# Two interleaved attentions: router units moved by one step, and within a step, in hand-written unit schedules

## The chip, the cores and the metric

The kernel runs on one core of one Trainium2 chip. The time is the device time of one execution, in microseconds (us). The engines are TensorE (PE in the profile; PEld is its weight load), VectorE (DVE), ScalarE (ACT), GpSimd (POOL) and the DMA-issuing SyncE (SP). Each works through its own instruction list; they meet only in semaphores.

## The reference

Sixteen sequences of 100 tokens with 256 features, and a context of 361 tokens for each, go through four residual blocks:

```python
x = x + tanh(g_xattn[0]) * L0_xattn(layernorm(x), ctx, ctx, mask)     # 16 heads of 16, softmax over 361 keys
x = x + tanh(g_ffn[0])   * L0_ffn(layernorm(x))      # 8 experts, top 2, capacity 1.25: logits, top_k, ranks, gather
x = x + tanh(g_xattn[1]) * L1_xattn(layernorm(x), ctx, ctx, mask2)    # 16 heads of 64, then a layer norm of its own
x = x + tanh(g_ffn[1])   * L1_ffn(layernorm(x))      # 8 experts, top 2 by gates
```

What matters here is that each attention is followed by a routing: normalised rows times router weights give eight logits a token, the two best experts are chosen, and the rank of each token within its expert (a running count over all tokens before it) says in which row of DRAM its features are stored for the expert stage.

## The kernel before

The program is a row of stages: norms, `attention_first` (some 45 to 427 us in the profile), `experts_first`, `attention_second` (some 725 to 1440 us), `experts_second`. Each attention treats eight pairs of batches. A pair is eight **steps** (plus some more in the last pair, where the pipeline runs out). The first pair and the last are written out, pairs 1 to 6 are a hardware loop.

In a step TensorE does the scores of four heads, **turns** (transposes) the four probability tiles of the step before, multiplies those of two steps before with the values (**value**), and, in between, **units**. A unit is one small product into a bank of its own, which another engine then takes away. The order of units is written by hand in `first_schedule` and `second_schedule`: a list of lists `at`, one for each step, with entries (kind, batch 0 or 1 of the pair, tile, part). Part -1 means: for the pair before this one. Kinds: Q, K, V projections; R spreads the softmax inverses, W is the output projection; N, G and C are the three routing units: N transposes the normalised rows (`Router.turn`, L225), G makes the router logits (`Router.score`, L237), C makes the ranks (`Router.rank_rows`, L277 and L278). "none" is an empty unit that makes the number of units a multiple of the banks (two in the first attention, three in the second).

All engines walk the same list. In a step of the first attention (`steps` of each engine) TensorE does: score, turns 0 and 1, value, unit 0, turn 2, unit 1, turn 3, all other units. In the second: score, turn 0, unit 0, turn 1, unit 1, turn 2, unit 2, value, turn 3, all other units. VectorE does four `find_max` (the row minima of the negated scores), then the routing's `moments` where they are due, then copies of finished values and takes the units in their order. Taking G includes `choose`: the maxima, their indices and the one-hot rows (L249 to L261), which C reads. ScalarE makes the exponentials and copies the turned tiles, takes the upper half of Q and K (a rounded copy; `lower` makes the rest), and calls `make_rows` (L215) at the end of the step that the routing is due in: the normalised rows that N transposes. GpSimd's part in the first attention, L1191 to L1211, is for each step: mask conversion, `lower` for each Q and K of the step, `router.scales` (inverse deviation and shift, L206 to L167) if routing is due, then for C `router.route` (15 small operations) and four scatters.

`ROUTE_AT` is the step of the first attention in which moments, scales and rows of the pair before are made (`routed_pair`, L1109). N follows one step later, G two. In the second attention the corresponding constant is `Z_AT`.

Every engine is in order, so a wait in it also holds whatever it has behind the waiting instruction. A score of the first attention also waits until VectorE has copied the value result of the step before (L1578), since both share a bank. A unit waits until the unit that used its bank before is taken.

Of the kernel before, what the change touches and what calls it, by code (L numbers as in the profile page):

```python
# [366 lines left out]
Z_AT = 3  # L367


def second_schedule(last):  # L370

    layer = Layer(1, 64, 1.0 / 16)
    at = [[] for _ in range(STEPS + LAG_VALUE + 5)]
    half = STEPS // 2
    for p in range(half):
        at[p] += [("K", 1, 2 * p, 0), ("K", 1, 2 * p + 1, 0)]
    parts = [(t, p) for t in range(KT_N) for p in range(2)]
    for m, (t, p) in enumerate(parts):  # L380
        at[(1, 1, 3, 3, 4, 4)[m]].append(("V", 1, t, p))
    at[LAG_VALUE].append(("W", 1, 0, -1))
    if not last:
        for p in range(half):
            at[half + p] += [("K", 0, 2 * p, 0), ("Q", 0, 2 * p, 0), ("K", 0, 2 * p + 1, 0), ("Q", 0, 2 * p + 1, 0)]
        for m, (t, p) in enumerate(parts):
            at[half + (1, 1, 2, 3, 3, 3)[m]].append(("V", 0, t, p))
    at[half + LAG_VALUE].append(("W", 0, 0, 0))
    for k, kind in enumerate("NGC"):
        at[Z_AT + 2 + k].insert(0 if kind == "C" else len(at[Z_AT + 2 + k]), (kind, 0, 0, -1))  # L390
    if last:
        at[STEPS + LAG_VALUE].append(("W", 1, 0, 0))
        for k, kind in enumerate("NGC"):
            at[STEPS + LAG_VALUE + 2 + k].append((kind, 0, 0, 0))
        return Units(layer, [u for slot in at for u in slot], at)
    at = at[:STEPS]
    for k in range(-sum(len(slot) for slot in at) % BANKS):
        at[k].append(("none", 0, k, 0))
    return Units(layer, [u for slot in at for u in slot], at)


def attention_second(nc, T, D_):
# [36 lines left out]
    ps_p = [ps(f"ps_p{k}") for k in range(BANKS)]  # L439

    full, final = second_schedule(False), second_schedule(True)
    half = STEPS // 2
    pre = Units(layer, [("Q", 0, t, 0) for t in range(H // 2)] + [("K", 0, t, 0) for t in range(H // 2)]
# [537 lines left out]
QUAD_TURN, QUAD_VALUE = 1, 2  # L981
QUAD_PB, QUAD_PT = 8, 8
FIRST_BANKS = 2
FIRST = 4
ROUTE_AT = 4


def first_schedule(last):

    layer = Layer(0, 16, 0.25)
    at = [[] for _ in range(QUADS + QUAD_VALUE + 5)]
    half = QUADS // 2
    at[0].append(("W", 0, 0, -1))
    at[1] += [("K", 1, 0, 0), ("V", 1, 0, 0)]
    at[2] += [("R", 1, 0, -1), ("V", 1, 1, 0)]
    at[3] += [("K", 1, 1, 0), ("V", 1, 2, 0), ("W", 1, 0, -1)]  # L1000
    at[ROUTE_AT + 1].append(("N", 0, 0, -1))
    at[half + QUAD_VALUE].append(("R", 0, 0, 0))
    at[ROUTE_AT + 2].append(("G", 0, 0, -1))
    if last:
        at[half + QUAD_VALUE + 1] += [("C", 0, 0, -1), ("W", 0, 0, 0)]
        at[QUADS + QUAD_VALUE].append(("R", 1, 0, 0))
        at[QUADS + QUAD_VALUE + 1].append(("W", 1, 0, 0))
        for k, kind in enumerate("NGC"):
            at[QUADS + QUAD_VALUE + 2 + k].append((kind, 0, 0, 0))
        return Units(layer, [u for slot in at for u in slot], at)  # L1010
    at[5] += [("K", 0, 0, 0), ("Q", 0, 0, 0)]
    at[6] += [("V", 0, 0, 0), ("V", 0, 1, 0)]
    at[7] += [("C", 0, 0, -1), ("K", 0, 1, 0), ("Q", 0, 1, 0), ("V", 0, 2, 0)]
    at = at[:QUADS]
    for k in range(-sum(len(slot) for slot in at) % FIRST_BANKS):
        at[ROUTE_AT].append(("none", 0, k, 0))
    return Units(layer, [u for slot in at for u in slot], at)


def attention_first(nc, T, D_):  # L1020
# [32 lines left out]
    ps_p = [ps(f"ps_p{k}") for k in range(FIRST_BANKS)]  # L1053

    full, final = first_schedule(False), first_schedule(True)
    half = QUADS // 2
    pre = Units(layer, [("Q", 0, 0, 0), ("K", 0, 0, 0), ("Q", 0, 1, 0), ("K", 0, 1, 0)]
# [51 lines left out]
    def routed_pair(i, p):  # L1109

        if p == ROUTE_AT:
            return None if isinstance(i, int) and i == 0 else i - 1
# [1481 lines left out]
```

How the kernel before makes its waits and increments, by code:

```python
def wait(eng, counted, i, k):  # L53
    value = counted.at(i, k)
    if not isinstance(value, int) or value > counted.per:
        eng.wait_ge(counted.sem, value)
# [13 lines left out]
    def link(self, eng, ins):  # L71
        eng.wait_ge(self.sem, self.mark(ins))
# [16 lines left out]
    def link(self, eng, ins):  # L89
        eng.wait_ge(self.sem, self.mark(ins))
# [78 lines left out]
    def z_scales(self, pool, j):  # L169
        g, r = self.nc.gpsimd, slice(0, S)
        pool.wait_ge(self.z_averaged.sem, self.z_averaged.at(j, 1))
        self.pool_own.link(pool, g.tensor_scalar(self.dev[r, :], self.mv[r, :, 1], 1e-30, None, ALU.max))
        self.pool_own.link(pool, self.power(self.dev, 0.5))
        self.pool_own.link(pool, g.tensor_scalar(self.rs[r, :], self.dev[r, :], (D / (D - 1.0)) ** 0.5, Z_EPS, ALU.mult, ALU.add))
        self.pool_own.link(pool, self.power(self.rs, -1.0))
        self.make_shift(pool, self.z_scaled)
# [1 line left out]
    def z_rows(self, act, j):  # L179
        act.wait_ge(self.z_scaled.sem, self.z_scaled.at(j, 1))
        self.apart(act)
        for s in range(2):
            z = self.T["xn"][0:S, bass.ds((2 * j + s) * D, D)]
            ins = self.nc.scalar.activation(z, z, ACT.Identity, scale=self.rs[0:S, s:s + 1], bias=self.shift[0:S, s:s + 1])
        ins.then_inc(self.z_done.sem, 1)
# [13 lines left out]
    def scales(self, pool, j):  # L200
# [1 line left out]
        g, r = self.nc.gpsimd, slice(0, S)  # L202
        if j:
            pool.wait_ge(self.dispatched, 64 * j)
        pool.wait_ge(self.averaged.sem, self.averaged.at(j, 1))
```

## Time and profile before

| | |
|---|---|
| median of 3 runs | 1630.07 us (1629.55 to 1630.86) |
| profiled execution, whole | 1641.7 us |
| its span, first to last instruction | 1639.9 us |
| TensorE matmul busy | 1338.0 us (82%) |
| VectorE / ScalarE / GpSimd busy | 876.4 / 802.0 / 409.4 us |
| mean granted TensorE clock | 0.908 of full speed |

Rows of a timeline give start, duration, engine, source line, operation, what is written and read, and how many instructions of the kind are merged; the bracket is the idle time of the engine before it and what ended it. The granted clock is 1.0 at 2.4 GHz; 0.5 is the level of 1.2 GHz.

### The profile page before, as it was taken

How to read it: one execution, taken by the hardware profiler on the slowest of the kernel's cores; microseconds unless marked ns; L12 is line 12 of the kernel's file. 1: busy time of each engine (PE TensorE's matmuls, PEld its weight loads, DVE VectorE, ACT ScalarE, POOL GpSimd, SP SyncE). 2: the span in 40 equal slices, each digit the busy share in tenths (PEclk: the TensorE clock that was granted, in tenths of full speed). 3: DMA queues.
4: the chain of work that ended last, by engine and by line, in shares of the span. 5: the costliest groups of instructions: out<-in, count | busy, mean ns of one | idle time of the engine just before them, and what ended most of it. 6: DMA issues, size and time to landing. Idle time of an engine off the chain costs nothing. (4 is left out here: it accounts for less than half of the span.)

```text
span 1639.9 us, 36347 instructions
## 1 busy us (share of the span) xinstructions
PE 1338.0 (82%) x10688; PEld 1063.1 (65%) x10689; DVE 876.4 (53%) x2927; ACT 802.0 (49%) x2195; POOL 409.4 (25%) x711
## 2 busy tenths in 40 slices
PE   2799999997299996179998999999999999369970
PEld 2566676665288886068777777777777876236650
DVE  3466666665254552537575656666665667122223
ACT  3577777776154452246463646455554545123320
POOL 2335545454200001620012111211212111300016
PEclk9899999999599999579999999999998998579995
DMA  5922212210333321220000000000000015111213
GB/s 126 414 87 89 86 52 88 80 47 22 113 117 146 127 98 36 70 81 22 11 12 12 11 21 11 13 19 10 21 10 21 1 36 206 67 38 64 64 58 108
DMA packets 47373, 111.35 MB, mean 68 GB/s; under 512 B 10828, under 2 KB 31500, under 8 KB 43468
## 3 DMA queue, kind: packets, MB, share of 16 engines
q1 hardware_dynamic: 37188, 96.25, 16.8%
q0 software_dynamic: 8192, 13.15, 2.9%
q10 hardware_dynamic: 1872, 0.68, 0.3%
q14 instruction: 86, 0.70, 0.1%
q8 instruction: 35, 0.57, 0.1%
HBM read 70.37 MB, written 43.84 MB: 70 GB/s over the span
## 5 line engine op out<-in xcount | busy, mean ns | idle before, releaser
L759 ACT ACTIVATE b_prob<-b_prob,b_low 100x361 f32<-100x361 f32 x256 | 154.8, 605 | 114.2 <-DVE b_low L871 114.2
L767 ACT COPY b_prob_t<-b_ps_t 128x300 f32<-128x300 f32 x256 | 103.4, 404 | 125.8 <-PE b_ps_t L672 123.1
L608 PE MATMUL b_ps_p<-b_context_part,b_wk_part 128*128 128x362 f32 x768 | 163.0, 351 | 0.0
L1413 ACT ACTIVATE a_prob<-a_prob,a_low 100x361 f32<-100x361 f32 x256 | 153.1, 600 | 6.9 <-DVE a_low L1547 6.9
L614 PE MATMUL b_ps_p<-b_wv_part,b_context_part 128*128 128x512 f32 (+1 forms) x576 | 151.5, 405 | 0.0
L871 DVE CUSTOM_DVE_ANT_0 b_prob<-b_ps_s,b_mask_bias 100x361 f32<-100x361 f32 x256 | 121.3, 530 | 39.7 <-PE b_ps_s L662 23.5
L672 PE MATMUL b_ps_t<-ident,b_prob 100*128 100x100 f32 x768 | 122.7, 271 | 23.8 <-ACT b_prob_t L767 23.2
L1547 DVE CUSTOM_DVE_ANT_0 a_prob<-a_ps_s,a_mask_bias 100x361 f32<-100x361 f32 x256 | 121.4, 531 | 36.3 <-PE a_ps_s L1314 36.3
L1421 ACT COPY a_prob_t<-a_ps_t 128x300 f32<-128x300 f32 x256 | 97.5, 406 | 80.4 <-PE a_ps_t L1324 78.5
L608 PEld LDWEIGHTS b_ps_p<-b_context_part,b_wk_part 128*128 128x128 f32 x768 | 129.1, 196 | 0.3 <-issue 0.2
L672 PEld LDWEIGHTS b_ps_t<-ident,b_prob 100*128 100x128 f32 x768 | 82.4, 147 | 67.2 <-issue 53.0
L614 PEld LDWEIGHTS b_ps_p<-b_wv_part,b_context_part 128*128 128x128 f32 (+1 forms) x576 | 100.7, 182 | 21.9
L809 DVE TENSOR_TENSOR b_keys_lo<-b_ps_p,b_keys_hi 128x361 fp32r<-128x361 f32 x128 | 68.2, 533 | 85.3 <-ACT b_keys_hi L748 85.3
L884 DVE TENSOR_SCALAR b_prob<-b_prob,b_inv 100x361 f32<-100x361 f32 x256 | 108.3, 423 | 2.2
L1324 PE MATMUL a_ps_t<-ident,a_prob 100*128 100x100 f32 x768 | 104.9, 263 | 2.0 <-ACT a_prob_t L1421 0.9
L1324 PEld LDWEIGHTS a_ps_t<-ident,a_prob 100*128 100x128 f32 x768 | 81.2, 147 | 35.0 <-issue 23.4
L1939 PE MATMUL f_ps<-f_w_part,f_ht 128*128 128x256 f32 x768 | 95.8, 284 | 7.6 <-DVE f_w_part L2029 7.6
L1939 PEld LDWEIGHTS f_ps<-f_w_part,f_ht 128*128 128x128 f32 x768 | 93.1, 192 | 9.1 <-issue 9.0
L1926 PE MATMUL f_ps<-f_xt,f_w_part 128*128 128x512 f32 x384 | 92.0, 399 | 4.1 <-DVE f_xt L2012 2.8
L694 PE MATMUL b_ps_s<-b_prob_t,b_values 128*64 128x100 f32 (+1 forms) x1536 | 87.8, 267 | 1.2 <-issue 1.2
L694 PEld LDWEIGHTS b_ps_s<-b_prob_t,b_values 128*64 128x64 f32 (+1 forms) x1536 | 74.8, 147 | 19.6 <-issue 19.3
L1926 PEld LDWEIGHTS f_ps<-f_xt,f_w_part 128*128 128x128 f32 x384 | 73.3, 193 | 20.6 <-issue 3.2
(295 smaller groups left out, 2650.5 us busy)
## 6 DMA issues: line engine op xcount, KB each, us to landing
rows_in<-zero SPq DMA_DIRECT2D x44, 512.0 KB, 4.8
w<-in_c_fc SPq DMA_DIRECT2D x8, 1024.0 KB, 5.7
w<-in_c_proj SPq DMA_DIRECT2D x8, 1024.0 KB, 5.0
a_context<-in_ctx SPq DMA_DIRECT2D x16, 361.0 KB, 3.5
b_context<-in_ctx SPq DMA_DIRECT2D x16, 361.0 KB
rows_in<-rows_in SPq DMA_DIRECT2D x8, 512.0 KB, 4.1
f_xe<-rows_in SPq DMA_DIRECT2D x8, 512.0 KB, 3.3
rows_out<-f_ye SPq DMA_DIRECT2D x8, 512.0 KB, 2.6
```

The source lines that it names most:

```text
L608: ins = nc.tensor.matmul(bank[:, 0:LN2], w_parts["k"][a][:, k, t * P:(t + 1) * P], cx_parts[s][b][:, k, :], start=m == 0, stop=m == DK * l ...
L614: ins = nc.tensor.matmul(bank[0:kn, :], cx_parts[s][b][:, k, k0:k0 + kn], w_parts["v"][a][:, k, p * 512:(p + 1) * 512], start=m == 0, stop ...
L672: ins = nc.tensor.transpose(ps_t[:, c * S:(c + 1) * S], prob[0:S, k % PAIR_PB, c * P:(c + 1) * P], T["ident"][0:S, 0:S])
L694: ins = nc.tensor.matmul(ps_o[g][64 * e:64 * e + 64, :], vt[b][0:kn, c, h * 64:h * 64 + 64], pt[0:kn, (2 * t + e) % PAIR_PT, c * S:(c + 1) ...
L759: nc.scalar.activation(prob[0:S, k, 0:L], prob[0:S, k, 0:L], ACT.Exp, bias=low[0:S, k:k + 1], scale=-1.0, accum_out=total[0:S, k:k + 1]).t ...
L871: nc.vector.tensor_tensor_reduce(out=prob[0:S, k, 0:L], in0=ps_s[g % 4][0:S, 0:L], in1=bias[s][0:S, :], scale=-layer.scale, scalar=BIG, op ...
L884: nc.vector.tensor_scalar(prob[0:S, k, 0:L], prob[0:S, k, 0:L], inv[0:S, k:k + 1], None, ALU.mult).then_inc(normed.sem, 1)
L1324: ins = nc.tensor.transpose(ps_t[k % 2][:, c * S:(c + 1) * S], prob[0:S, k % QUAD_PB, c * P:(c + 1) * P], T["ident"][0:S, 0:S])
L1413: nc.scalar.activation(prob[0:S, k, 0:L], prob[0:S, k, 0:L], ACT.Exp, bias=low[0:S, k:k + 1], scale=-1.0, accum_out=total[0:S, r:r + 1]).t ...
L1547: nc.vector.tensor_tensor_reduce(out=prob[0:S, k, 0:L], in0=ps_s[g % FIRST][0:S, 0:L], in1=bias[s][0:S, :], scale=-layer.scale, scalar=BIG ...
L1926: ins = nc.tensor.matmul(ps[2 + f % 2][:, :], w1_parts[a][:, k, f * P:(f + 1) * P], xt[b][:, k, :], start=m == 0, stop=m == DK * len(PASSE ...
L1939: ins = nc.tensor.matmul(ps[4 + j % 2][:, 0:D], ht[a][:, f, j * P:(j + 1) * P], w2_parts[b][:, f, :], start=m == 0, stop=m == NF * len(PAS ...
```

## The change

In the first attention, the output projection W of the pair before (batch 1) goes from the end of step 3 to step 4, where it is alone. `ROUTE_AT` goes from 4 to 5: moments, scales and rows are made in step 5, N in step 6, G in step 7. C stays in step 7 but goes from the front of the step to its end. In the last pair C changes places with W in step 7. The empty unit goes from step 4 to step 0. In the second attention, G goes from the end of step 6 to its third place, and C from first to second place in step 7.

```diff
@@ second_schedule
     for k, kind in enumerate("NGC"):
-        at[Z_AT + 2 + k].insert(0 if kind == "C" else len(at[Z_AT + 2 + k]), (kind, 0, 0, -1))
+        at[Z_AT + 2 + k].insert((len(at[Z_AT + 2]), 2, 1)[k], (kind, 0, 0, -1))
@@
-ROUTE_AT = 4
+ROUTE_AT = 5
@@ first_schedule
-    at[3] += [("K", 1, 1, 0), ("V", 1, 2, 0), ("W", 1, 0, -1)]
+    at[3] += [("K", 1, 1, 0), ("V", 1, 2, 0)]
+    at[4].append(("W", 1, 0, -1))
     at[ROUTE_AT + 1].append(("N", 0, 0, -1))
     at[half + QUAD_VALUE].append(("R", 0, 0, 0))
     at[ROUTE_AT + 2].append(("G", 0, 0, -1))
     if last:
-        at[half + QUAD_VALUE + 1] += [("C", 0, 0, -1), ("W", 0, 0, 0)]
+        at[half + QUAD_VALUE + 1] += [("W", 0, 0, 0), ("C", 0, 0, -1)]
@@
-    at[7] += [("C", 0, 0, -1), ("K", 0, 1, 0), ("Q", 0, 1, 0), ("V", 0, 2, 0)]
+    at[7] += [("K", 0, 1, 0), ("Q", 0, 1, 0), ("V", 0, 2, 0), ("C", 0, 0, -1)]
     at = at[:QUADS]
     for k in range(-sum(len(slot) for slot in at) % FIRST_BANKS):
-        at[ROUTE_AT].append(("none", 0, k, 0))
+        at[0].append(("none", 0, k, 0))
```

The units of pairs 0 to 6, worked out from the two functions (a minus marks the pair before; the digit is the batch):

```
first     step 0       1       2       3          4       5            6            7
before    W0-          K1 V1   R1- V1  K1 V1 W1-  none    N- K0 Q0     R0 G- V0 V0  C- K0 Q0 V0
after     W0- none     K1 V1   R1- V1  K1 V1      W1-     K0 Q0        N- R0 V0 V0  G- K0 Q0 V0 C-

second    step 5                        6                             7
before    K0 Q0 K0 Q0 V0 V0 N-          K0 Q0 K0 Q0 V0 W0 G-          C- K0 Q0 K0 Q0 V0 V0 V0
after     K0 Q0 K0 Q0 V0 V0 N-          K0 Q0 G- K0 Q0 V0 W0          K0 C- Q0 K0 Q0 V0 V0 V0
```

The last pair of the second attention comes out as before.

## Rows read from the trace of the kernel before

**Rows 1.** Windows (start:end, length, busy time of each engine, clock, DMA share, GB/s).
```profile
50.00:404.00 354.00, 320.42 (x3732) 235.43 (x3732) 227.23 (x857) 263.39 (x826) 162.04 (x283) 0.96 0.28 101
205.40:212.30 6.90, 6.87 (x54) 4.96 (x55) 2.74 (x10) 4.61 (x14) 1.10 (x3) 0.53 0.00 1
```
**Rows 2.** Timeline, TensorE, first attention, pair 4 from step 3 on: score starts.
```profile
239.50 0.41 PE L1314 MATMUL a_ps_s<-a_keys_hi,a_queries_hi 32*100 32x362 f32 x4
244.50 1.89 PE L1288 MATMUL a_ps_p<-wo,a_out_t 128*100 128x256 f32 x8
246.32 0.41 PE L1314 MATMUL a_ps_s<-a_keys_hi,a_queries_hi 32*100 32x362 f32 x4
250.94 0.42 PE L1314 MATMUL a_ps_s<-a_keys_hi,a_queries_hi 32*100 32x362 f32 x4 [0.93 <-DVE a_out_t L1578]
256.56 0.41 PE L1314 MATMUL a_ps_s<-a_keys_hi,a_queries_hi 32*100 32x362 f32 x4
262.35 0.41 PE L1314 MATMUL a_ps_s<-a_keys_hi,a_queries_hi 32*100 32x362 f32 x4
268.60 0.41 PE L1314 MATMUL a_ps_s<-a_keys_hi,a_queries_hi 32*100 32x362 f32 x4
273.32 0.41 PE L1314 MATMUL a_ps_s<-a_keys_hi,a_queries_hi 32*100 32x362 f32 x4
```
**Rows 3.** Timeline, TensorE, pair 3: scores of step 5 and step 6.
```profile
205.43 0.63 PE L1314 MATMUL a_ps_s<-a_keys_hi,a_queries_hi 32*100 32x362 f32 x4 [0.92 <-DVE a_out_t L1578]
213.35 0.42 PE L1314 MATMUL a_ps_s<-a_keys_hi,a_queries_hi 32*100 32x362 f32 x4
```
**Rows 4.** Timeline, ScalarE, pair 5, step 1: upper half of K.
```profile
278.94 0.50 ACT L1397 CAST a_keys_hi<-a_whole_keys 128x361 fp32r<-128x361 f32 x1
```
**Rows 5.** Timeline, pair 4: scales, N; then GpSimd's K and Q, and R.
```profile
250.25 0.50 POOL L206 TENSOR_SCALAR a_rs<-a_mv 100x2 f32<-100x2 f32 x1 [0.87 <-DVE a_mv L155]
253.64 0.54 PE L225 MATMUL a_ps_p<-ident,a_rows 100*128 100x100 f32 x4 [0.34 <-ACT a_rows L215]
257.52 0.95 POOL L1176 TENSOR_TENSOR a_keys_lo<-a_whole_keys,a_keys_hi 128x361 fp32r<-128x361 f32 x1 [5.34 <-ACT a_keys_hi L1397]
258.91 0.56 PE L1282 MATMUL a_ps_p<-ident,a_inv_wide 100*128 100x100 f32 x4
259.83 0.85 POOL L1121 TENSOR_TENSOR a_queries_lo<-a_query_part,head_rows 128x400 fp32r<-128x400 f32 x1
```
**Rows 6.** Timeline, last pair, step 1: K's upper half, and GpSimd's subtraction.
```profile
367.48 0.50 ACT L1397 CAST a_keys_hi<-a_whole_keys 128x361 fp32r<-128x361 f32 x1
373.82 0.96 POOL L1176 TENSOR_TENSOR a_keys_lo<-a_whole_keys,a_keys_hi 128x361 fp32r<-128x361 f32 x1
```
**Rows 7.** Timeline, GpSimd, end of the first attention: scales of the last pair.
```profile
407.50 0.23 POOL L206 TENSOR_SCALAR a_rs<-a_mv 100x2 f32<-100x2 f32 x1 [1.81 <-DMA rows_in<-a_rows,a_scat]
```
**Rows 8.** Groups, TensorE, 780 to 1420 us: busy, mean ns, idle before.
```profile
L237 PE MATMUL b_ps_p<-wr,b_rows_t 128*100 128x8 f32 x56 | 5.5, 225 | 0.0
...
L277 PE MATMUL b_ps_p<-b_either,earlier 100*128 100x16 f32 x14 | 2.7, 271 | 11.2 <-DVE b_either L261 11.2
```
**Rows 9.** Timeline, TensorE, second attention, step 7: score, turns 1 and 3; pair 0.
```profile
1138.05 0.41 PE L662 MATMUL b_ps_s<-b_keys_hi,b_queries_hi 64*100 64x362 f32 x2
1143.22 0.45 PE L672 MATMUL b_ps_t<-ident,b_prob 100*128 100x100 f32 x3 [1.07 <-ACT b_prob_t L767]
1148.33 0.48 PE L672 MATMUL b_ps_t<-ident,b_prob 100*128 100x100 f32 x3
...
795.96 0.41 PE L662 MATMUL b_ps_s<-b_keys_hi,b_queries_hi 64*100 64x362 f32 x2 [0.26 <-issue]
799.56 0.74 PE L672 MATMUL b_ps_t<-ident,b_prob 100*128 100x100 f32 x3 [1.97 <-ACT b_prob_t L767]
```
**Rows 10.** The same, pair 4, step 6: turns 1 and 3.
```profile
1127.83 0.45 PE L672 MATMUL b_ps_t<-ident,b_prob 100*128 100x100 f32 x3
1131.45 0.48 PE L672 MATMUL b_ps_t<-ident,b_prob 100*128 100x100 f32 x3
```

## The prediction

> A measurement of this kernel resolves about 0.2%, 3.3 us; "same" means within that.
>
> **What bounds the kernel now.** I read the windows by stage first. In the steady part of the first attention TensorE is busy 320 of 354 us, ScalarE 263, VectorE 227; TensorE's granted clock averages 0.96 [rows 1]. The second attention looks alike. So time is lost or won in three ways only: TensorE waits, half-clock stretches, and a changed order that turns waits into work. Next I read TensorE's timeline from one start of the score matmul (L1314) to the next, which cuts a pair into its eight steps. Pair 4 gives step 3 = 246.32-239.50 = 6.82, step 4 = 250.94-246.32 = 4.62, step 5 = 5.62, step 6 = 5.79, step 7 = 6.25, and step 0 of pair 5 is 4.72 [rows 2]. Step 3 holds three units, step 4 none, and after step 4 the score waits 0.93 for VectorE. In pairs 3 and 5 step 5 takes 7.92 instead of 5.62 [rows 3]; its granted clock is 0.53 [rows 1], the half-rate level.
>
> **First attention, the output projection.** W (pair before, batch 1) leaves step 3 and becomes step 4's only unit. Step 3 without it: its other work ends at 244.50, where W starts, and the score comes about 0.1 later, so 244.50-239.50+0.1 = 5.1. Step 4 with it is step 0's twin (one W, the softmax inverses, nothing else): 4.72 [rows 2]. Saved per pair: 11.44-9.82 = 1.6; the idle of step 4 is what hides it. The empty unit costs one semaphore; I take 0, bound 0.2 per pair.
>
> **First attention, the routing one step later.** This is the expensive part. Step 4 had no K or Q. Step 5 has K and Q of the next pair, and GpSimd's code (L1195 to L1200) runs `lower` for them before `router.scales`. So the scales queue behind two splits; ScalarE waits for them in `make_rows`, with step 6's copies and exponentials queued behind; TensorE waits for the rows in N, with the rest of step 6 queued behind. From the start of step 5:
> - K is now the first unit, as in step 1, where ScalarE's upper half of K starts 278.94-273.32 = 5.6 in [rows 2, 4].
> - The cast takes 0.50 [rows 4], a handover some 0.15 (estimate): GpSimd starts the lower half at 6.2. From there to the end of the second query mask: 259.83+0.85-257.52 = 3.2, so 9.4 [rows 5].
> - From the first scale to N: 253.64-250.25 = 3.4 [rows 5], so N at 12.8.
> - Step 6 reaches its first unit (R before, N now) 258.91-256.56 = 2.35 after its score [rows 2, 5], and step 5 without N takes 5.1 like the new step 3: N is wanted at 7.45. New wait: 5.3.
> - The old step 6 took 262.35-258.91 = 3.4 from R on [rows 2, 5]. G leaves it (5.5/7 = 0.79 each [rows 8], some 0.65 of it not overlapped), N brings 0.4. So step 7 starts at 12.8+3.4-0.65+0.4 = 16.0. Steps 5 and 6 took 11.4: +4.55.
> - Step 7 gets G first and C last: G for C in front +0.2; the choice on VectorE now delays K's pickup, and so V's bank, by 0.2; C at the end 0.45. Estimates from the same units' lengths, +0.85.
>
> Can GpSimd take the scales first? In the last pair ScalarE casts K at 367.48, yet GpSimd's subtraction starts at 373.82, with no idle before it: it stood behind the routing and four scatters [rows 6]. The Trainium skill, TensorE: Matmul & The Clock Gate, section on the array's architectural detail, calls GpSimd's queue strict first-in-first-out; the row agrees. By that rule the sum is the one below; with a queue that could reorder it would be the faster rival.
>
> The clock: after gaps of 0.93 and less it fell in two loop pairs; a gap of 5.3 should do it every time. The price lies between 1.7 and 3.3 (the 2.8 to 3.2 after N, doubled, in part or with some of step 7). I take the row for such a stretch, 7.92-5.62 = 2.3 [rows 2, 3]. The two old drops (4.6) go with step 4's gaps.
>
> Per loop pair -1.6+4.55+0.85+2.3 = +6.1; six pairs +36.6, less 4.6 = +32. Pair 0 has no such units. The last pair has no K or Q in step 5 and gains some 1.5 there. But its C comes behind W (1.89 [rows 2]), W's VectorE work and G, about 3.8 later in the step (estimate), and the four scatters of C are what its last scales already wait 1.81 for [rows 7]: +1.5 net. First attention: **+33.5**. Bounds: +26 (wait 4.8, clock 1.7) and +43 (wait 5.8, clock 3.3).
>
> **Second attention.** TensorE waits 11.2 us before C in six places (L277) [rows 8]. G ends step 6; VectorE must finish W's four operations and the choice before step 7's first `find_max`, which holds ScalarE's first exponential and copy, and with them turn 1: it starts 1143.22-1138.05 = 5.17 into step 7, itself after 1.07 of wait [rows 9]. Now the choice falls into step 6, beside value and K; G moves within step 6, and V, the next user of its bank, needs only the logits copied, so the step's length stays. In step 7 the first unit is K, which needs nothing new, and C comes after turn 1, its input long there. When can turn 1 start? Pair 0 has no choice, only W in front of `find_max`: 799.56-795.96 = 3.60 [rows 9]. From turn 1 to turn 3, step 6 takes 1131.45-1127.83 = 3.62 for Q, K, value and a turn [rows 10]; step 7 does the same work in 1148.33-1143.22 = 5.11 [rows 9]. I read the 1.5 between them as half clock (the turn in pair 0 takes 0.74, at full clock 0.45). New: 3.62 less K (some 1.2), plus C (0.6) and 0.2 for the next copy = 3.2. Turn 3 comes at 6.8 instead of 1148.33-1138.05 = 10.28: -3.5. In pair 0 K fills the gap of 1.97 and its own slow stretch can go; I put it at 3.5 too. Seven pairs: **-24.5**. The last pair's order stays.
>
> Bounds: if the clock still falls (some 0.95 of wait remains before turn 1), each gains 3.5-1.5 = 2.0, so -14; if some pairs now lose more than 1.5 to the clock, -27. C's rank work on GpSimd ends about 0.5 later; next in its queue are a context split and the scales of step 3, and nobody waits for them by then.
>
> **Sum.** The profiled execution took 1641.7 (span 1639.9); both attentions are serial stages in it. The median of the runs is 1630.07, 11.6 lower, and I apply the difference to that: 1630.1+33.5-24.5 = **1639.1**.
>
> **Rivals.**
> - The clock still falls in the second attention (-14): 1630.1+33.5-14 = 1649.6. For it: drops after gaps of 0.93 and less [rows 2, 3]. Against: the gaps shrink from 1.87+1.07 to 0.95+0.2. Slower, chance 0.17.
> - The same page of the skill, in Part 1, lets the clock fall after an idle spell and keeps it while TensorE is busy; by it a remaining 0.95 would not count and this rival would go. The drops of rows 3 speak the other way, so it keeps its chance.
> - The first costs its low end (+26) and the second gains fully (-27): 1629, with all up to 1633 no change, 0.15. For it: a slow stretch that falls mostly where ScalarE is catching up.
> - Faster than before: GpSimd has the scales ready while TensorE is still in step 5, so no new wait. Steps 5 and 6 then give 5.1+2.35+3.4-0.65+0.4 = 10.6, -0.8, and no clock price: 6x(-1.6-0.8+0.85)-4.6+1.5 = -12.4, and 1630.1-12.4-24.5 = 1593. What decides is the place in the queue: rows for N at 7.45 need the first scale by 7.45-3.4 = 4.05, before K is even cast (5.6). Chance 0.06; smaller errors on this side make faster 0.11.
>
> The forecast itself (slower, 1633 to 1645) has 0.45; the high end of the first attention (+43, 1648.6) 0.12. Slower in all 0.74, same 0.15, faster 0.11. The range of 1628 to 1653 holds the low case, the clock rival and the high end.
>
> **What would show it.** After: TensorE waits about 5 us for ScalarE's rows before N (L225) in six pairs of the first attention, and ScalarE for GpSimd's shift (L167); steps 3 and 4 are 5.1 and 4.7; the 0.93 before step 5's score is gone; half clock follows N. In the second, L277's 11.2 is gone and turn 3 of step 7 stands at 6.8. A short wait before N would prove the main step wrong; a turn 3 at 8.3 would mean the clock rival.

## The result

Medians of the runs taken together: before 1630.46 us (4 runs, 1629.55 to 1634.1), after 1649.01 us (4 runs, 1647.48 to 1653.85). The ratio is 1.0115, 95% interval 1.0089 to 1.0141: the change costs 18.5 us. The forecast was +9.0 and 1639.1 us. The time went up as forecast and lies inside the stated range of 1628 to 1653; the size of the change, 18.5 for 9.0, was wrong.

| | before | after |
|---|---|---|
| profiled execution | 1641.7 | 1647.48 |
| span | 1639.9 | 1645.7 |
| mean granted clock | 0.908 | 0.915 |
| first attention: first score to first expert product | 390.5 | 423.0 |
| second attention: first projection to first score | 27.9 | 33.4 |
| second attention: first score to last C | 690.1 | 657.5 |

The stages are differences of start times on TensorE's timeline. Source lines after the edit are one higher in the first attention (L1314 becomes L1315).

The two profiled executions are only 5.8 us apart, the medians 18.5. The profile after agrees with nearly every step of the working, and yet the time doesn't agree with the sum; the sections below ask why. The projections of the second attention, which the change leaves alone, took 26.8 to 33.4 over all profiles here, so the 5.5 in that row are not put down to the change.

**First attention after the change.** TensorE, pair 4, score starts of steps 3 to 7 and of step 0 of the next pair, with N and a V between:

```profile
256.51 0.41 PE L1315 MATMUL a_ps_s<-a_keys_hi,a_queries_hi 32*100 32x362 f32 x4
261.60 0.41 PE L1315 MATMUL a_ps_s<-a_keys_hi,a_queries_hi 32*100 32x362 f32 x4
266.31 0.41 PE L1315 MATMUL a_ps_s<-a_keys_hi,a_queries_hi 32*100 32x362 f32 x4
271.35 0.42 PE L1315 MATMUL a_ps_s<-a_keys_hi,a_queries_hi 32*100 32x362 f32 x4
278.67 0.90 PE L225 MATMUL a_ps_p<-ident,a_rows 100*128 100x100 f32 x4 [4.96 <-ACT a_rows L215]
281.03 2.67 PE L1267 MATMUL a_ps_p<-wv,a_context 128*128 128x256 f32 x8
283.63 0.41 PE L1315 MATMUL a_ps_s<-a_keys_hi,a_queries_hi 32*100 32x362 f32 x4
290.63 0.51 PE L1315 MATMUL a_ps_s<-a_keys_hi,a_queries_hi 32*100 32x362 f32 x4
```

Steps 3, 4, 5 are 5.09, 4.71, 5.04; the 0.93 of [rows 2] before a score is gone; step 6 is 12.28 with a wait of 4.96, and step 7 is 7.00. Step 6 varies from 11.98 to 13.28 over the six loop pairs. The same stretch on GpSimd and ScalarE:

```profile
272.44 0.97 POOL L1177 TENSOR_TENSOR a_keys_lo<-a_whole_keys,a_keys_hi 128x361 fp32r<-128x361 f32 x1 [6.06 <-ACT a_keys_hi L1398]
273.36 0.62 POOL L1181 TENSOR_TENSOR a_query_part<-a_whole_queries,a_query_part 128x200 fp32r<-128x200 f32 x1
273.93 0.86 POOL L1122 TENSOR_TENSOR a_queries_hi<-a_query_part,head_rows 128x400 fp32r<-128x400 f32 x1
274.74 0.86 POOL L1122 TENSOR_TENSOR a_queries_lo<-a_query_part,head_rows 128x400 fp32r<-128x400 f32 x1
275.56 0.23 POOL L206 TENSOR_SCALAR a_rs<-a_mv 100x2 f32<-100x2 f32 x1
...
277.03 0.19 POOL L167 TENSOR_TENSOR a_shift<-a_shift,a_rs 100x2 f32<-100x2 f32 x1
277.44 1.09 ACT L215 ACTIVATE a_rows<-x,a_shift,a_rs 100x256 f32 x2 [3.75 <-POOL a_shift L167]
```

GpSimd idles 6.06, then does the four operations of the splits of K and Q, and only then comes to the scales (L206), with no gap ahead of them. ScalarE stands 3.75 before the rows. TensorE's windows (length, busy times of PE, PEld, DVE, ACT, POOL, then the granted clock), from the score of step 5 to N and from N to step 7, put the half-rate stretch behind N:

```profile
266.31:278.67 12.36, 7.02 (x99) 4.98 (x99) 6.15 (x25) 7.93 (x25) 4.60 (x9) 0.88 0.12 47
278.67:283.63 4.96, 4.96 (x22) 4.28 (x23) 1.57 (x3) 3.61 (x12) 0.00 (x0) 0.61 0.00 0
```

The waits over the whole execution (total, times, longest). The first row is six times 4.96 in the loop, 1.04, and 9.4 behind the last pair:

```profile
PE a_ps_p L225 <- ACT a_rows L215: 40.2, 8, 9.4
...
ACT a_rows L215 <- POOL a_shift L167: 34.8, 7, 12.3
```

**Second attention after.** TensorE's groups from 775 to 1433 us (busy, mean ns, idle before): L277's idle of 11.2 [rows 8] is 2.0.

```profile
L277 PE MATMUL b_ps_p<-b_either,earlier 100*128 100x16 f32 x16 | 2.8, 253 | 2.0 <-DVE b_either L261 2.0
```

Step 7 of a pair, score, turn 1, C, turn 2, turn 3, and the next score:

```profile
1162.90 0.41 PE L662 MATMUL b_ps_s<-b_keys_hi,b_queries_hi 64*100 64x362 f32 x2
1166.64 0.45 PE L672 MATMUL b_ps_t<-ident,b_prob 100*128 100x100 f32 x3 [1.07 <-ACT b_prob_t L767]
1166.93 0.33 PE L277 MATMUL b_ps_p<-b_either,earlier 100*128 100x16 f32 x2
1167.68 0.45 PE L672 MATMUL b_ps_t<-ident,b_prob 100*128 100x100 f32 x3 [0.20 <-ACT b_prob_t L767]
1169.95 0.48 PE L672 MATMUL b_ps_t<-ident,b_prob 100*128 100x100 f32 x3
1176.17 0.41 PE L662 MATMUL b_ps_s<-b_keys_hi,b_queries_hi 64*100 64x362 f32 x2
```

Turn 1 comes at 3.74 after the score (5.17 before [rows 9]), turn 3 at 7.05 (10.28 before; forecast 6.8). The step takes 13.27 where it took 16.5. The wait of 1.07 before turn 1 is the one of [rows 9]; it has not shrunk. In pair 2 the clock falls after the same two waits (granted clock 0.69 from 1002 to 1004 us, 0.50 from 1004 to 1006). Value, turn 3 and the start of K run at half rate, and the step takes 14.78:

```profile
1000.73 0.45 PE L672 MATMUL b_ps_t<-ident,b_prob 100*128 100x100 f32 x3 [1.07 <-ACT b_prob_t L767]
1001.77 0.45 PE L672 MATMUL b_ps_t<-ident,b_prob 100*128 100x100 f32 x3 [0.21 <-ACT b_prob_t L767]
1002.87 2.27 PE L694 MATMUL b_ps_s<-b_prob_t,b_values 128*64 128x100 f32 x24
1005.07 0.76 PE L672 MATMUL b_ps_t<-ident,b_prob 100*128 100x100 f32 x3
```

### The profile page after: what moved, and what is told of

It is laid out like the page before. It is cut to its first block and busy times, and to the rows that moved or that the text cites. A ratio compares the mean times of both kernels' runs of the same rounds, so it can differ in the third digit from the quotient of the medians.

```text
span 1645.7 us, 36347 instructions
## 1 busy us (share of the span) xinstructions
PE 1325.3 (81%) x10688; PEld 1054.1 (64%) x10689; DVE 880.2 (53%) x2927; ACT 801.2 (49%) x2195; POOL 407.8 (25%) x711
## 5 line engine op out<-in xcount | busy, mean ns | idle before, releaser
L608 PE MATMUL b_ps_p<-b_context_part,b_wk_part 128*128 128x362 f32 x768 | 158.0, 343 | 0.0
L1548 DVE CUSTOM_DVE_ANT_0 a_prob<-a_ps_s,a_mask_bias 100x361 f32<-100x361 f32 x256 | 121.4, 531 | 39.7 <-PE a_ps_s L1315 37.1
L871 DVE CUSTOM_DVE_ANT_0 b_prob<-b_ps_s,b_mask_bias 100x361 f32<-100x361 f32 x256 | 121.2, 530 | 36.9 <-PE b_ps_s L662 21.8
L672 PE MATMUL b_ps_t<-ident,b_prob 100*128 100x100 f32 x768 | 118.0, 263 | 24.6 <-ACT b_prob_t L767 23.9
L608 PEld LDWEIGHTS b_ps_p<-b_context_part,b_wk_part 128*128 128x128 f32 x768 | 124.9, 190 | 0.2 <-issue 0.2
L672 PEld LDWEIGHTS b_ps_t<-ident,b_prob 100*128 100x128 f32 x768 | 78.4, 142 | 68.8 <-issue 52.3
L1325 PEld LDWEIGHTS a_ps_t<-ident,a_prob 100*128 100x128 f32 x768 | 82.8, 147 | 37.1 <-issue 24.9
L694 PE MATMUL b_ps_s<-b_prob_t,b_values 128*64 128x100 f32 (+1 forms) x1536 | 83.5, 259 | 1.2 <-issue 1.2
L694 PEld LDWEIGHTS b_ps_s<-b_prob_t,b_values 128*64 128x64 f32 (+1 forms) x1536 | 70.8, 140 | 16.7 <-issue 15.9
```

Of the source, the lines that this page charges most:

```text
L608: ins = nc.tensor.matmul(bank[:, 0:LN2], w_parts["k"][a][:, k, t * P:(t + 1) * P], cx_parts[s][b][:, k, :], start=m == 0, stop=m == DK * l ...
L672: ins = nc.tensor.transpose(ps_t[:, c * S:(c + 1) * S], prob[0:S, k % PAIR_PB, c * P:(c + 1) * P], T["ident"][0:S, 0:S])
L694: ins = nc.tensor.matmul(ps_o[g][64 * e:64 * e + 64, :], vt[b][0:kn, c, h * 64:h * 64 + 64], pt[0:kn, (2 * t + e) % PAIR_PT, c * S:(c + 1) ...
L871: nc.vector.tensor_tensor_reduce(out=prob[0:S, k, 0:L], in0=ps_s[g % 4][0:S, 0:L], in1=bias[s][0:S, :], scale=-layer.scale, scalar=BIG, op ...
L1325: ins = nc.tensor.transpose(ps_t[k % 2][:, c * S:(c + 1) * S], prob[0:S, k % QUAD_PB, c * P:(c + 1) * P], T["ident"][0:S, 0:S])
L1548: nc.vector.tensor_tensor_reduce(out=prob[0:S, k, 0:L], in0=ps_s[g % FIRST][0:S, 0:L], in1=bias[s][0:S, :], scale=-layer.scale, scalar=BIG ...
```

## The experiments

**The theory going in**: both parts do what the working says. The first costs because the scales queue in GpSimd behind two splits, and the second gains because the choice is no longer ahead of the first `find_max`. The rivals: something else in the first part costs (ScalarE's own queue, the place of W), or the second part gives less than its stage shows.

### Both kernels again, and each part alone

`e3_second_only` has the edit in `second_schedule` alone, `e4_first_only` all the others alone:

```diff
-        at[Z_AT + 2 + k].insert(0 if kind == "C" else len(at[Z_AT + 2 + k]), (kind, 0, 0, -1))
+        at[Z_AT + 2 + k].insert((len(at[Z_AT + 2]), 2, 1)[k], (kind, 0, 0, -1))
```

> The kernel before, once more. The profiled execution of before took 1641.7 us and the median of its runs 1630.07, while the two times of the changed kernel (1647.5 and 1649.0) agree. Theory (the base was off): a fresh profile of before takes 1630 to 1635, and the 5 to 12 us that it is shorter lie in stretches whose order the change doesn't touch or in half-clock stretches of the second attention (711 us from its first score to the next stage in the old profile, 700 to 705 now). Rival (the profile costs before 11 us each time): it takes about 1641 again, with the same stage lengths.

> The changed kernel once more. Both theories: 1647 to 1651. Its first attention takes 423 us from the first score to the first expert product, as in its first profile (390.5 before). The 33.4 us from the second attention's first projection to its first score, 27.9 before, tell whether that 5.5 belongs to the change: if it was chance, a second profile shows another value between 27 and 34.

> Only the second attention's change (G third in step 6, C second in step 7); the first attention is that of before. My working: seven pairs at 3.5 less, 1630-24 = 1606. If the old profile had more half clock in the second attention than the timed runs have, less is to be gained: 1610 to 1618. If the two parts of the change hinder each other (rival), this alone gives 1606 or less and the first part alone less than 33 over before.

> Only the first attention's change. My working: +33.5, so 1630+33.5 = 1663. Rival (part of the cost arises behind the first attention, in loads or in the norm before the second): 1668 or more. The ratios of this run and of the one with the second part alone should multiply to that of the whole change if the parts are independent.

Measured, against the kernel before on the same chip (1665.89 us): before again 1670.27 us, 1.0037 [0.9999, 1.0075]; after 1671.36, 1.0046 [1.0007, 1.0084]; second part alone 1648.93, 0.9906 [0.9873, 0.9939], or -15.7 us; first part alone 1690.73, 1.0161 [1.0091, 1.0230], or +26.8. The signs of the two parts are as forecast, but all four times were missed by 20 us and more: this chip takes 36 us more for the kernel before. There the whole change costs 7.7 us by its ratio, and 1.1 beside e1. In the profile of e1, step 3 of the first attention, 6.82 in [rows 2], takes 8.1 to 12.3 in pairs 2 to 7. Pair 4, end of step 2 and start of step 3, all engines (some rows left out):

```profile
244.46 1.14 POOL L322 DMA_INDIRECT rows_in<-a_rows,a_scat  x1 [0.92 <-POOL a_scat L316]
...
245.91 0.99 POOL L322 DMA_INDIRECT rows_in<-a_rows,a_scat  x1 [0.30 <-issue]
...
247.20 0.99 POOL L322 DMA_INDIRECT rows_in<-a_rows,a_scat  x1 [0.30 <-issue]
247.95 0.26 DVE L1578 COPY a_out_t<-a_ps_s 128x100 f32<-128x100 f32 x1 [2.28 <-remote]
...
248.27 0.41 PE L1314 MATMUL a_ps_s<-a_keys_hi,a_queries_hi 32*100 32x362 f32 x4 [1.28 <-issue]
...
248.74 0.41 ACT L1421 COPY a_prob_t<-a_ps_t 128x300 f32<-128x300 f32 x1 [2.75 <-remote]
...
252.58 2.78 PE L1261 MATMUL a_ps_p<-a_context,wk 128*128 128x361 f32 x4
...
259.36 0.42 PE L1314 MATMUL a_ps_s<-a_keys_hi,a_queries_hi 32*100 32x362 f32 x4
```

VectorE, TensorE and ScalarE idle together while GpSimd issues its four indirect scatters. VectorE's copy had its input long before: it stands 2.28 though the value product ended at 245.1. TensorE's score waits for that copy by the kernel's own order. Then TensorE's clock falls (granted 0.54 from 250 to 254 us; K takes 2.78, at full rate 1.48), and step 3 is 259.36-248.27 = 11.1. I call this the stall. It is in neither profile of the first measurement.

### The queue, and the next wait behind it

`e7_scales_first` changes one thing in the changed kernel: GpSimd makes the scales before the splits.

```diff
-                    for u, unit in sched.slots[p]:
-                        if unit[0] in ("Q", "K"):
-                            lower(unit, sched.split[u], i, False)
...
+                    for u, unit in sched.slots[p]:
+                        if unit[0] in ("Q", "K"):
+                            lower(unit, sched.split[u], i, False)
```

`e8_rows_early` adds to that ScalarE's rows moved forward in its step, to behind the third exponential.

```diff
+                    if j is not None and p < QUADS:
+                        router.make_rows(act, j)
...
-                    if j is not None:
+                    if j is not None and p >= QUADS:
```

> The kernel before again, to see on whatever chip this runs how long its stages are beside those of the next three. Two profiles of it so far took 390.5 and 418.3 us from the first score to the first expert product of the first attention; the second had steps 2 and 3 of its pairs at 5.6 and 8 to 12 instead of 4.2 and 6.8, with TensorE, VectorE and ScalarE all idle at once. If that is a property of the chip, all kernels of this call show it or none does; if it is chance, it is spread among them.

> The changed kernel. Theory: steps 4 to 7 of the first attention's loop are the same on every chip (4.71, 5.04, 12 to 13.3, 7.0 so far) and only steps 2 and 3 change. The time over before then depends on how much the common stalls of steps 2 and 3 take in each of the two: 18 us where there are none, 5 to 8 where there are.

> The changed kernel, but GpSimd makes the routing's scales ahead of the two splits in a step of the first attention (one block of lines moved). Theory (the wait before N is GpSimd's queue): scales start about 3.4 into step 5 instead of 9.2, ScalarE's rows then follow its last exponential at 7.4, N comes at 8.6 instead of 12.3, a wait of about 1.2 instead of 5.0, and the clock stays up. Step 6 falls from 12 to 13.3 to about 6.7: 6 us in each of six pairs, 36 us less than the changed kernel. Rival (the chain from moments to rows is itself too long for one step): step 6 stays above 9, and less than 20 us come back.

> As the last one, and ScalarE makes the rows right after the third exponential of step 5 instead of at its end. Theory: rows at 6.5 instead of 7.4 into step 5, N at 7.7, a wait of 0.4 left: another 0.8 in each of six pairs, 5 us less than with the scales first alone. If the next wait is elsewhere (Q's upper half now comes 1.1 later, and with it GpSimd's masks), it gives nothing or up to 3 us back.

All four profiles of this chip show the stall. Measured against 1673.11 us: before 0.9989 [0.9951, 1.0027]; after 1.0011 [0.9986, 1.0037]; scales first 0.9778 [0.9741, 0.9815]; rows early 0.9768 [0.9719, 0.9816]. Scales first is 1637.83 us, 37.8 below after (1675.62). In its profile step 6 is 6.58 or 6.59 in all six pairs, from 12.0 to 13.3. One of them, GpSimd and TensorE:

```profile
262.52 0.23 POOL L206 TENSOR_SCALAR a_rs<-a_mv 100x2 f32<-100x2 f32 x1 [3.30 <-DVE a_mv L155]
...
265.27 0.96 POOL L1177 TENSOR_TENSOR a_keys_lo<-a_whole_keys,a_keys_hi 128x361 fp32r<-128x361 f32 x1 [1.09 <-ACT a_keys_hi L1398]
...
264.18 0.41 PE L1315 MATMUL a_ps_s<-a_keys_hi,a_queries_hi 32*100 32x362 f32 x4
267.64 0.53 PE L225 MATMUL a_ps_p<-ident,a_rows 100*128 100x100 f32 x4 [1.10 <-ACT a_rows L215]
270.76 0.41 PE L1315 MATMUL a_ps_s<-a_keys_hi,a_queries_hi 32*100 32x362 f32 x4
```

The scales now stand 2.75 ahead of the split, in time in which GpSimd was idle before, and N waits 1.10 instead of 4.96. So the cost is the place in GpSimd's queue, shown by its removal. The remaining 1.10 did come from ScalarE's rows being at the end of their step: with the rows moved forward it is 0.27. But step 6 is 6.49, a gain of 0.09 where 0.8 was expected. The trace of e8 shows where the rest went, TensorE, pair 4, N and turn 2 (the score of step 6 is at 263.46):

```profile
266.08 0.53 PE L225 MATMUL a_ps_p<-ident,a_rows 100*128 100x100 f32 x4 [0.26 <-ACT a_rows L215]
267.21 0.45 PE L1325 MATMUL a_ps_t<-ident,a_prob 100*128 100x100 f32 x3 [0.60 <-ACT a_prob_t L1422]
```

Turn 2 now waits 0.60 for ScalarE's copy of the turned tiles. That copy starts 3.22 after the score in e7 and in e8 alike (267.40-264.18 and 266.68-263.46), with no idle time of ScalarE between score and copy in either: the rows are the same work in its queue, before or behind the exponentials.

### The stall: scatters taken away

`e11_plain_stores` is the kernel before with the four indirect scatters of a pair in the first attention replaced by four plain stores of the same size to fixed rows. The first experts then get other rows than the routing asks for.

```diff
+        if self.n == 0:
+            self.calls = getattr(self, "calls", -1) + 1
+            for m in some:
+                first = (4 * self.calls + m) * S
+                pool.dma_start(rows_in[first:first + S, :], self.rows[0:S, (m % 2) * D:(m % 2 + 1) * D]
+                               ).then_inc(self.dispatched, 16)
+            return
```

> The kernel before. If this chip shows no common stall in steps 2 and 3 of the first attention (4.2 and 6.8 in all pairs), the median should be near 1630, as at first, and its profile tells which stage is shorter than in the profile of 1641.7: by the later profiles I expect the second attention (684 us from its first score to its last ranks instead of 690) and the first attention's step 5 without the two half-clock pairs (5.6 instead of 7.9, 386 us instead of 390.5). If it shows the stall, 1660 to 1675.

> The changed kernel. On a chip without the stall 1647 to 1650, 16 to 20 more than before; on a chip with it 1668 to 1677, 2 to 8 more than before, since the pairs of before lose 4 to 5 us in steps 2 and 3 and those of after 3 to 4.

> The kernel before, with the four indirect scatters of a pair in the first attention replaced by four plain stores of the same size to fixed rows, so that the first experts get other rows than the routing asks for; everything else as before. Theory (the stall comes with GpSimd's scatters, which run from 11 to 17 us into the next pair, in its steps 2 and 3): steps 2 and 3 fall to 4.2 and 6.8 in every pair on a chip where the kernel before has 5.6 and 8 to 12, 20 to 28 us less in all. Rival (it is in the loop's code, in TensorE, VectorE or ScalarE waiting for instructions): they stay as in before.

> Only the second attention's change. From the profiles so far: 684 to 690 us from the first score to the last ranks become 660 to 663, so 23 to 24 us less than before wherever it runs, 0.986. The first time it gave 0.9906 beside a before that scattered by 30 us; if that was the true size, some of the 24 is given back outside the second attention.

Measured against 1675.9 us: before 0.9987 [0.9948, 1.0027]; after 1.0002 [0.9975, 1.0029]; plain stores 0.9729 [0.9680, 0.9778], 45 us less where 20 to 28 were expected; second part alone 0.9848 [0.9804, 0.9892]. With plain stores, step 3 is 6.82 or 6.83 in all loop pairs and step 2 is 4.2: the stall comes with the scatters. Not all of the 45 us is the stall, though. The profiled executions of e9 and e11, on this chip, are 26.2 apart, as much as their first attentions (412.8 and 386.5), and within what was expected; the rest of the 45 is in executions without a profile. And behind the last score of the last pair the stores save time too: from there to the first expert product it is 49.4 to 51.0 us in the kernel before with scatters and 44.8 with stores. Part of that is TensorE's wait for the expert's rows, first profile and e13 (the same kernel as e11, below):

```profile
440.44 1.97 PE L1916 MATMUL f_ps<-ident,f_xe 128*128 128x128 f32 x8 [23.97 <-DMA f_xe<-rows_in]
...
435.33 1.97 PE L1923 MATMUL f_ps<-ident,f_xe 128*128 128x128 f32 x8 [20.85 <-DMA f_xe<-rows_in]
```

In e12 pairs 2 to 6 all show the stall and a second drop of the clock. TensorE, pair 4, score starts from step 2: step 3 takes 10.99, and after the old gap of 0.93 step 5 takes 7.97, where 5.6 is the usual length.

```profile
251.23 0.42 PE L1314 MATMUL a_ps_s<-a_keys_hi,a_queries_hi 32*100 32x362 f32 x4
256.88 0.41 PE L1314 MATMUL a_ps_s<-a_keys_hi,a_queries_hi 32*100 32x362 f32 x4 [1.39 <-DVE a_out_t L1578]
267.87 0.42 PE L1314 MATMUL a_ps_s<-a_keys_hi,a_queries_hi 32*100 32x362 f32 x4
272.49 0.63 PE L1314 MATMUL a_ps_s<-a_keys_hi,a_queries_hi 32*100 32x362 f32 x4 [0.93 <-DVE a_out_t L1578]
280.46 0.42 PE L1314 MATMUL a_ps_s<-a_keys_hi,a_queries_hi 32*100 32x362 f32 x4
```

### The change without the stall

Both kernels with plain stores, on one chip with both originals.

> The kernel before, with the four indirect scatters of each pair in the first attention replaced by four plain stores to fixed rows (the first experts get other rows in another order, so the output isn't the reference's). Beside plain_after below, it measures the change with the stall of steps 2 and 3 out of the way. Theory: first attention 386 to 388 us, second to its last choice 683 to 690, its time 0.97 to 0.98 of the kernel before, as when it first ran. The rival, that its gain of 45 us was a chance of one set of runs: 0.985 or more.

> The changed kernel with the same plain stores. Theory: the change costs the same steps as in the first two profiles (step 6 at 12 to 13.3, step 7 of the first attention at 7.0, step 7 of the second at 13.3), and with no stall in either kernel it adds 32 to the first attention (418 to 422) and takes 24 from the second: its time is 8 to 11 us over e13_plain_before (ratio of the two 1.005 to 1.007). Rival: the first measurement's +18.5 is the change without the stall, and the profile hides part of it: then 16 to 21 us over e13_plain_before, ratio 1.010 to 1.013. Second rival: the stall also took time in the first two sets that no profile showed, and the two lie within 4 us.

> The changed kernel beside the kernel before on this chip. If the stall of steps 2 and 3 is there (step 3 over 8 us in most pairs of the kernel before), 1.000 to 1.005, as in the other three calls; if this chip doesn't show it (step 3 at 6.82), the difference is that of e14_plain_after less e13_plain_before: by the theory +8 to +11 us (1.005 to 1.007), by the rival +16 to +21 (1.010 to 1.013).

> The kernel before, for a profile on this chip: whether step 3 is 6.82 or 8 to 12 here, and how far its profiled execution lies from the median of its runs (11.6 us above in the first profile, of which the prediction took the difference to hold). If the first attention takes 386 to 391 and the second 684 to 686 to its last choice, with a median near 1630, the first profile was one with some 5 us more in the second attention than the runs have; ratio to the kernel before 1.000 within 0.003.

Measured against 1671.06 us: plain before 1631.28 us, 0.9761 [0.9716, 0.9806]; plain after 1650.86, 0.9873 [0.9828, 0.9918]; after 1672.21, 0.9999 [0.9967, 1.0032]; before 1676.23, 1.0031 [0.9999, 1.0064]. Without the stall the change costs 19.6 us, as in the first measurement (18.5) and against my theory of 8 to 11: the rival was right. With the stall, on the same chip, it costs nothing that these intervals resolve. With all fast executions of the kernel before on a chip taken together (28 to 34), the mean of after is 4.8, 3.3, 3.1 and 1.5 us above it on the four chips, each within 3 to 4: some 3 us in all. Taking the scatters away is worth 40 us to the kernel before and 21 to the one after.

Both profiled executions of the plain kernels lie within 0.2 us of their medians, so here the stages may be subtracted: 1.9 before the first score, +35.7 in the first attention, -17.8 in the second, -0.2 in the rest, together +19.6. TensorE's score starts of steps 3, 4 and 5 in the kernel before with plain stores, pair 4, give 6.83 and 4.61 for steps 3 and 4, as in [rows 2], and 6.43 for step 5:

```profile
240.55 0.41 PE L1321 MATMUL a_ps_s<-a_keys_hi,a_queries_hi 32*100 32x362 f32 x4
247.38 0.41 PE L1321 MATMUL a_ps_s<-a_keys_hi,a_queries_hi 32*100 32x362 f32 x4
251.99 0.41 PE L1321 MATMUL a_ps_s<-a_keys_hi,a_queries_hi 32*100 32x362 f32 x4 [0.93 <-DVE a_out_t L1585]
258.42 0.41 PE L1321 MATMUL a_ps_s<-a_keys_hi,a_queries_hi 32*100 32x362 f32 x4
```

### Each part without the stall

> The first attention's part of the change alone, with the plain stores of e13 (its output isn't the reference's, as there). Beside e13 (1631.3) and e14 (1650.9, so +19.6 for both parts). By the working (+33.5 and -24.5, together +9) and the profiles' stages (422 and 684 to 687): 1665 to 1667. Of the 10 us that both parts together cost more than the forecast, this run and the next tell where they are: if in the first attention, 1672 to 1676; if in the second, 1665. Rival: the first part's cost was mis-sized by less than 3 us, and the second gives 5 or more less than forecast.

> The second attention's part alone, with the plain stores of e13. By the working 1606 to 1608 (-24.5); by the stages of the profiles (685.5 to 661.7) 1607 to 1609; if the part gives only what e13 and e14 show between them (680.8 to 663.0, -18), 1613 to 1615. If the two parts' differences from 1631.3 add to +18 to +21, they are independent; if they add to +8 to +12, the parts disturb each other when together.

Measured on a further chip: first part 1662.58 us (1655.22 to 1667.78), second part 1609.53 (1607.17 to 1613.11), 53.05 apart where the forecast has 33.5+24.5 = 58. Against the 1631.28 of e13, on another chip, that is +31.3 and -21.8, together +9.5. Against the kernel before on each chip (ratios 0.9977 and 0.9671, over e13's 0.9761) it is +36 and -15, together +21. The forecasts were 1665 to 1667 for the first part (2.4 above what came) and 1607 to 1609 or 1613 to 1615 for the second. Absolute times of two chips can't tell these apart, and by times alone whether the parts disturb each other stays open. The stages do tell:

| kernel | first attention | second attention |
|---|---|---|
| before, first profile | 390.5 | 690.1 |
| before with plain stores, e11 / e13 | 386.5 / 386.2 | 683.9 / 680.7 |
| first part alone, plain, e17 | 422.4 | 679.5 |
| second part alone, plain, e18 | 384.4 | 663.4 |
| after, first profile | 423.0 | 657.5 |
| after with plain stores, e14 | 422.0 | 663.0 |
| before with scatters, e1 / e5 / e9 / e16 | 418.3 / 413.1 / 412.8 / 423.3 | 684.2 / 686.5 / 685.8 / 686.8 |
| after with scatters, e2 / e6 / e10 / e15 | 449.0 / 453.0 / 449.6 / 450.4 | 660.2 / 663.5 / 660.7 / 663.2 |
| first part alone, scatters, e4 | 444.2 | 684.2 |
| second part alone, scatters, e3 / e12 | 419.7 / 435.0 | 662.6 / 659.7 |

With plain stores the first attention goes from 385.7 (mean of e11, e13, e18) to 422.2 (e14, e17), whatever the second is, and the second from 681.4 (e11, e13, e17) to 663.2 (e14, e18), whatever the first is: +36.5 and -18.2, together +18.3. The parts are independent there. Both differences hold something that is not the edit's size: behind the last score of the last pair the first attention grows by 4.7 with plain stores and by 2.3 to 2.7 with scatters, and the second attention from its last score to the last C, whose order the change leaves, takes 39.0 to 39.2 in e11, e13 and e17 but 41.3 and 41.4 in e14 and e18, by other lengths of half clock (its range over all profiles is 36.2 to 41.4, in both orders).

## Why the prediction was right in direction and wrong in size

- **W moved.** Steps 3 and 4 forecast at 5.1 and 4.72, found at 5.09 and 4.71; the empty unit's price is within its bound (it went to step 0, below).
- **Scales behind the splits.** Wait before N forecast 5.3, found 4.96; N at 12.8 from the start of step 5, found 278.67-266.31 = 12.36; the score of step 7 at 16.0 plus up to 2.3 of clock, found 283.63-266.31 = 17.3, and up to 18.3. e7 showed the cause. The Trainium skill's strict first-in-first-out queue on GpSimd (TensorE: Matmul & The Clock Gate, architectural detail) agrees: the scales started at 275.56, with the four operations of the two splits ahead of them in the list, though nothing they need came in between.
- **Step 7** forecast 6.25+0.85 = 7.1, found 7.00.
- **Steps 0 and 1**: not forecast. They are 0.4 and 0.2 longer (5.1 for 4.72, 5.42 for 5.21), +0.6 a pair, some 3.5 in all. C at the end of step 7 and the empty unit are candidates; neither was tried alone.
- **First attention as a whole**: 390.5+33.5 = 424.0 forecast, 423.0 found. The 33.5 is already less 4.6 for the two old drops of the clock in step 5. Without the drops the stage of the kernel before is 385.9, the forecast is +38.1 and what was found is +37.1. (The stage with plain stores, 385.7, has almost this number for another reason: some drops of its own in step 5, and 4.6 us less behind the last pair's last score. The low bound, stated as +26, is 26.9 by its own terms, which changes nothing.)
- **Second attention**: turn 3 forecast at 6.8, found 7.05, so 3.27 a pair (16.54 to 13.27) instead of 3.5. Pair 0 forecast 3.5; it goes from 15.0 (e13; 16.31 in the first profile) to 13.04, so 1.9. And the clock rival came true in part: the clock still falls in one or two pairs of an execution, 18 of 77 over the eleven profiles that have this part, each at 1.5, or 2.5 an execution. Together 6x3.27+1.9-2.5 = 19.0 instead of 24.5: this term was 5.5 too large. The stages fall by 18.2 with plain stores and by some 24 with scatters (685.8 to 661.9 on the mean of four each); the kernel before has more half clock in step 7 of pairs 1 and 2 and elsewhere in some executions than in others, so they scatter around the 19.0.
- **The base.** This is the step that failed first: "The median of the runs is 1630.07, 11.6 lower, and I apply the difference to that". The working had given the 4.6 of the two drops back to the change, as time that the changed kernel no longer loses; the 11.6 that were then subtracted hold the same 4.6. From the profiled execution itself the sum was 1641.7+9 = 1650.7, and the changed kernel's median is 1649.01. The excess of that execution can be found where stretches that should be alike differ, each at a mean granted clock of 0.59 to 0.83: step 5 of two pairs at 7.92 for 5.62 (4.6); pair 6 of the second attention with steps 0 and 1 at 9.20 and 10.16 where pair 3 has 7.70 and 8.81 (2.9); pair 0's step 7 at 16.31 for 15.0 (1.3); and steps 5, 6 and what is behind them in the last pair, 4.3 more than the mean of the plain-store profiles of that order. That is some 13, near the 11.6. An execution has more or fewer of such stretches. A difference built on an execution with extra drops, which the change partly takes away, holds for that execution and not for the median.
- **The two misses together**: +9.0, plus 4.6 (drops given back and subtracted as well), plus 5.5 (second attention), less 1.0 (first attention) is +18.1; the medians gave +18.5. This is an estimate from steps of these profiles. That the executions of 1630 had few half-clock stretches is worked out, and not shown: no profile of such an execution exists.
- **Right by luck**: two of the prediction's cases name nearly the measured 1649.0, the clock rival (1649.6) and the high end of the first attention (1648.6). Neither happened: the clock fell in 18 of 77 steps and not in all, and the first attention cost no more than forecast.
- **What none of this explains** is the difference between chips. On five other chips the kernel before took 1663.5 to 1675.9 us. On the four of them where both originals ran, after took 1.0046, 1.0011, 1.0002 and 0.9999 of it. The scatters cause the stall (e11, e13). Why the first measurement had no stall in either profile, and why taking the scatters away saves the kernel before 40 us and the changed one 21, is open. The profiles with scatters show 31 and 28 in the first attention (416.9 and 450.5 on the mean, less 385.7 and 422.2), of which 5.9 and 3.6 are behind the last score. They are also not middle executions: the four of the kernel before took 3.3 to 10.5 us less than their medians, and those of after between 1.5 less and 7.4 more. By profiles the change costs 11 us with the stall, by medians some 3; so part of the 40 lies in executions that no profile shows. One that lost more is e12, with the old order in the first attention and 435.0 there, 49 more than with plain stores; its step 5 at 7.97 behind the gap of 0.93, which the new order doesn't have, is a candidate that was not tried by itself.
- **Rivals.** Faster (0.06), by scales made in time, was the mechanism of e7: it needs an edit that the change doesn't have. Its sum, 36.9 less than before, came out at 35.3 (1637.83 for 1673.11) on a chip with the stall, with steps 5 and 6 at 11.6 for the 10.6 of the sum. "No change" is nearly what a chip with the stall measures, for a reason that was not among the cases. The Trainium skill has two passages on this in Part 1 of the same page. By the one that the prediction used, the clock falls after an idle spell and stays while TensorE is busy, which I read as that small waits would not count; the other, on a second failure mode, has the clock swing between its levels where TensorE idles briefly between groups of matmuls. These profiles fit the second better: of the 66 step 7s of pairs 1 to 6, 48 keep the full clock behind waits of 1.07 and 0.21, and 18 lose it behind the same waits, nine of them in pair 1. A price of 1.5 in one or two pairs would have been the right entry.

## What to carry to other kernels

Before a difference is built on a profile that lies above its median, find where the excess sits: set like stages of a loop side by side, and count the half-clock stretches among them. Those belong to that execution; don't give them back to the change and subtract them from the base as well. And see whether a profiled execution is a middle one of its kernel before two of them are subtracted.

A step that goes one later in a hand-written order queues in every engine that walks the order. Here a step's delay cost 5 us of wait a pair and the clock behind it, for the splits of K and Q in GpSimd's list, and moving the short operations of the scales ahead of them brought 37.8 us back. The version with both parts of the change and the scales first, 1637.83 us on a chip where the kernel before takes 1673.11 (0.9778), beats both kernels.

## What the runs showed of the hardware

- While GpSimd issued indirect scatters, VectorE, TensorE and ScalarE stood idle together, 2.28, 1.28 and 2.75 us in the execution shown; TensorE's part is its wait for VectorE's copy. Plain stores of the same size, issued by GpSimd too, took this away: step 3 of the first attention is 6.83 with them and 8.1 to 12.7 in pairs 2 to 7 of the kernel before without. The kernel before became 40 to 45 us faster by them (medians), some 6 of it behind the last pair's last score. Four chips show the stall in their profiles; in the two profiles of the first measurement it is absent, with the same scatters. What makes the engines stand is not shown.
- Behind the same short waits the clock sometimes falls and sometimes doesn't: 18 of 66 times behind 1.07 and 0.21, nine of the eleven times in pair 1 and nine of 55 in the others, with value at 2.27 for 1.26 and the step at 14.8 for 13.27; behind 0.84 and 0.59, in pair 0, never in eleven. Behind a wait of 4.96 it fell in all six pairs of each of the eight profiles that have it (granted clock 0.50 to 0.67 in the 4.96 us after N).
